# The recurrent loop of a layer: the LSTM moved to another phase of the step, with its high products ahead of the outer products, its gates ahead of tanh, its h ahead of the mask, and a copy by ScalarE

## The chip, the cores and the metric

The kernel runs on 1 core of one Trainium2 chip. The metric is the time of the device, in microseconds: the median of the kernel before is 2966.37 us over 3 runs (2957.95 to 2966.97).

The engines of the core are named as in the profile: PE (TensorE, matmuls), PEld (its weight loads), DVE (VectorE), ACT (ScalarE), POOL (GpSimd) and SP (SyncE, which here only issues DMAs). Each takes its instructions in the order in which they are written, and waits on semaphores.

## The reference

The kernel computes four layers on x of 8 sequences, 256 steps and 128 features. The change touches one stage of the third layer, which holds three recurrences over the 256 steps, each fed by the one before it:

```python
# L2_cond: LSTM, z = x Wx + b + h Wh, for each of 256 steps
i, f, o = sigmoid(ai), sigmoid(af), sigmoid(ao);  g = tanh(ag)
c = f * c + i * g
h = o * tanh(c)

# L2_attn: delta rule with 8 heads of 32, on xp = silu(h W_in^T)
kn        = k / (norm(k) + 1e-6)
delta     = v - S kn
S         = tanh(beta * S + outer(delta, kn))
Sq        = S q;   out = Sq * silu(Sq)        # y = out W_out^T, x = x + y

# L2_cond2: plain recurrence on the new x
h2 = tanh(h2 Wh2 + x Wx2 + b2)
```

## The kernel before

The stage is `recurrent_stages`. The 256 steps are cut into 16 waves of 16 steps (TC). The program runs in bodies of 16 steps: in body k the LSTM works on wave k, the projections (keys, values, beta, queries) on wave k-1, the delta rule on wave k-2, its output on wave k-3 and the plain recurrence (rnn) on wave k-4. So bodies 0 and 1 have the LSTM alone, bodies 2 to 15 have LSTM and delta rule, bodies 4 to 15 have everything, bodies 16 and 17 have the delta rule without the LSTM, and bodies 18 and 19 the rnn. The order on each engine is that of the program text: a loop over body and step on each engine, and inside it the calls of this step. What follows names lines of before.

- PE, a step of a full body: `retrieve` (L429, S times kn and q into `d_ps`), `rnn_product` (L406), `unread(o_ps)` (L448, a product that nobody reads), `spread_delta` (L441, the outer products into `o_ps`), `lstm_products` (L390, 24 bf16 products: h is split in three bf16 parts, the weights too), every eighth step a bias and the inputs of the rnn (L360, L400), `lstm_pieces` (L365, the inputs of the LSTM), `project` (L455 to L480), `output` (L490), `unread(d_ps)` (L448), `values` (L415, the v of the next step into `d_ps`).
- DVE: `masked` (L800, reads `d_ps`, writes `rows`; below a step is counted from the start of this instruction, called M), `lstm_h` (L772) and `split_h` (L785 to L794: h once more into PSUM, the rest, the middle part, the low part) for the LSTM step before, `summed` (L808, two halves), `project` and `output` (pieces of these stages), `lstm_cell` (L762, L765) for this LSTM step.
- ACT: `project` and `output`, `rnn_tanh` (L563), `new_state` (L556, two halves of S), `lstm_gates` (L546, L547), `lstm_tanh` (L551).
- POOL: `kept` (L649, beta times S, two halves), then pieces of `project` (norms, `kn_tok` L702, the spreading of kn and q L670).
- SP: for each body the stores of beta, kn and v to memory and their loads in another layout. `values` of a body's first step waits for `v_loaded`, the last part of this chain.

Of the kernel before, what the change touches and what calls it, by code (L numbers as in the profile page):

```python
# [9 lines left out]
BF16 = mybir.dt.bfloat16  # L10
ALU = mybir.AluOpType
# [7 lines left out]
P = 128  # L19
# [241 lines left out]
def recurrent_stages(nc, tag, x, y, wx, wh, bias, w_in, w_tok, w_q, beta_bias, w_out, sel_v, mask_r, mask_k, mask_q, mask_l, gate_sel,  # L261
# [8 lines left out]
    with ExitStack() as stack:  # L270
# [3 lines left out]
        h_rest, h_mid, h_low = mem.sb("h_rest", [P, WIDE]), mem.sb("h_mid", [P, WIDE], BF16), mem.sb("h_low", [P, WIDE], BF16)  # L274
# [34 lines left out]
                 "cell_ready", "tanh_ready", "h_ready", "rest_ready", "h_psum", "rest_psum", "mid_h_ready", "low_ready", "xin_psum", "xp_sig_ready", "xp_ready",  # L309
# [20 lines left out]
        def rnn_at(n, count=1):  # L330
            half, slot = (1, n % TC - 1) if 1 <= n % TC <= TCH else (0, (n - TCH - 1) % TC)
            at = (4 * TCH + slot) * B
            return lstm_ps[half][:, at:at + count * B]
# [18 lines left out]
        with nc.Block() as block:  # L352

            @block.tensor
            def _(pe):
# [14 lines left out]
                def lstm_pieces(w, step, rnn):  # L370
# [9 lines left out]
                def lstm_products(n):  # L380
                    alone = n <= IN_BANK
                    if not alone:
                        pe.wait_ge(s["low_ready"], n + 1)
                    h_parts = high(h_ring[:, (n - 1) % SLOTS, :]), high(h_rest[:, :]) if alone else h_mid[:, :], h_low[:, :]
                    for m in range(3):
                        if alone:
                            pe.wait_ge(s[("h_ready", "rest_ready", "low_ready")[m]], n + 1)
                        for g in range(4):
                            for k in range(3 - m):
                                last = nc.tensor.matmul(lstm_at(n, g, g + WIDE // B), w_part[k][:, g * P:(g + 1) * P],  # L390
                                                        h_parts[m], start=False, stop=(m == 2), skip_group_check=True)
                    last.then_inc(s["gates_psum"], 1)

                def rnn_inputs(w, lo, hi):
                    if lo == 0:
                        pe.wait_ge(s["x_added"], w + 1)
                        pe.wait_ge(s["r_ready"], w * TC + 1)
                    if lo == 1:
# [2827 lines left out]
```

## Time and profile before

| | |
|---|---|
| median of 3 runs | 2966.37 us |
| profiled execution | 2981.45 us, of which the span is 2979.7 us |
| mean granted TensorE clock | 0.821 |
| busy | PE 83%, PEld 59%, DVE 58%, ACT 37%, POOL 25% of the span |
| the stage of the change | about 1255 to 2180 us of the span |

The span runs from the first to the last instruction. The slices of the page show PE busy at 8 or 9 tenths through this stage, with the granted clock at 9 (full) up to about 2085 us and at 5 to 6 after it. PE's busy time counts pipelined matmuls from start to modelled end, so it isn't PE at its peak. The chain that the page follows back from the end lies in the last layer and says nothing on this stage.

### The profile page before, as it was taken

What the parts mean: (1) busy time and instruction counts of PE and PEld (TensorE: products, weight loads), DVE (VectorE), ACT (ScalarE), POOL (GpSimd) and SP (SyncE); (2) the same over time, 40 slices, a digit from 0 to 9 for tenths busy, and PEclk for the clock granted to TensorE, in tenths of its full rate; (3) what the DMA queues carried; (4) which work ended last, traced back from release to release, by engine and by line L of the source; (5) the groups of instructions that cost most, each with busy time, mean ns of one, the idle gap of its engine ahead of it and who ended that gap; (6) DMA issues with size and microseconds to landing.
All of it is one profiled execution on the core that took longest, in us unless ns stands there. A gap on an engine that the chain in (4) does not pass through costs nothing. (4 is left out here: it accounts for less than half of the span.)

```text
span 2979.7 us, 92693 instructions
## 1 busy us (share of the span) xinstructions
PE 2485.5 (83%) x37349; PEld 1762.4 (59%) x37354; DVE 1725.2 (58%) x7330; ACT 1105.3 (37%) x3986; POOL 750.8 (25%) x1227
## 2 busy tenths in 40 slices
PE   5998888882799889778888888889956878999998
PEld 3556666662455566555666666665534556777774
DVE  3553555556354544347777877776343865566675
ACT  1332333333133223224555555555244433333332
POOL 2210000000221000126666666767333310000000
PEclk9996555555699779889999999999556975898999
DMA  2000000001000000123534343435010000000000
GB/s 89 2 3 2 2 2 2 2 2 39 1 2 2 1 0 0 67 48 92 111 95 108 97 106 98 107 96 115 30 43 1 2 1 2 2 3 2 2 3 15
DMA packets 110106, 103.98 MB, mean 35 GB/s; under 512 B 90496, under 2 KB 90496, under 8 KB 108800
## 3 DMA queue, kind: packets, MB, share of 16 engines
q1 hardware_dynamic: 109696, 98.24, 13.1%
q8 instruction: 291, 4.77, 0.7%
q14 instruction: 119, 0.97, 0.1%
HBM read 89.81 MB, written 8.39 MB: 33 GB/s over the span
## 5 line engine op out<-in xcount | busy, mean ns | idle before, releaser
L649 POOL TENSOR_TENSOR l2r_beta_s<-l2r_state,l2r_beta_f 128x256 f32<-128x256 f32 x512 | 366.1, 736 | 274.8 <-ACT l2r_state L556 265.4
L556 ACT ACTIVATE l2r_state<-l2r_pre 128x256 f32<-128x256 f32 x512 | 191.6, 417 | 220.3 <-DVE l2r_pre L808 218.6
L808 DVE TENSOR_TENSOR l2r_pre<-l2r_o_ps,l2r_beta_s 128x256 f32<-128x256 f32 x512 | 193.1, 418 | 35.2 <-PE l2r_o_ps L441 33.1
L140 PE MATMUL l0r_bank<-main_x,l0r_wx_half 128*128 128x32 f32 (+2 forms) x480 | 150.0, 413 | 60.5 <-ACT l0r_out_gate L196 59.9
L140 PEld LDWEIGHTS l0r_bank<-main_x,l0r_wx_half 128*128 128x128 f32 x480 | 118.7, 311 | 81.7 <-ACT l0r_out_gate L196 79.5
L1801 PEld LDWEIGHTS l3r_bank<-main_x,l3r_wx_half 128*128 128x128 f32 x480 | 98.1, 231 | 93.2 <-issue 49.4
L441 PE MATMUL l2r_o_ps<-l2r_rows,l2r_outer 32*128 32x128 f32 x2048 | 134.1, 333 | 4.6 <-DVE l2r_rows L800 4.1
L194 ACT ACTIVATE l0r_gates<-l0r_bank 128x24 f32<-128x24 f32 x256 | 48.9, 191 | 237.0 <-PE l0r_bank L152 237.0
L1940 ACT ACTIVATE l3r_gates<-l3r_bank 128x24 f32<-128x24 f32 x256 | 48.9, 191 | 232.2 <-PE l3r_bank L1813 232.1
L228 DVE SCALAR_TENSOR_TENSOR l0r_both<-l0r_gates 128x16 f32<-128x16 f32 x256 | 44.8, 175 | 152.4 <-ACT l0r_gates L194 152.4
L152 PE MATMUL l0r_bank<-l0r_h_ring,l0r_w_part 128*128 128x8 bf16 x2304 | 102.6, 170 | 35.7 <-DVE l0r_h_ring L238 28.0
L1784 POOL TENSOR_SCALAR main_y<-l3r_h_ring 128x128 f32<-128x128 f32 x16 | 8.5, 530 | 481.9 <-DVE l3r_h_ring L2094 481.9
L152 PEld LDWEIGHTS l0r_bank<-l0r_h_ring,l0r_w_part 128*128 128x128 bf16 x2304 | 81.5, 105 | 68.4 <-DVE l0r_h_ring L238 65.0
L124 POOL TENSOR_SCALAR main_y<-l0r_h_ring 128x128 f32<-128x128 f32 x16 | 10.3, 645 | 441.8 <-DVE l0r_h_ring L238 441.8
L800 DVE TENSOR_TENSOR l2r_rows<-l2r_d_ps,main_even_layers 128x128 f32<-128x128 f32 x257 | 74.8, 291 | 80.5 <-PE l2r_d_ps L429 75.4
L448 PE MATMUL l2r_d_ps<-l2r_w_part 128*128 128x384 bf16 x384 | 120.8, 359 | 0.0
L441 PEld LDWEIGHTS l2r_o_ps<-l2r_rows,l2r_outer 32*128 32x128 f32 x2048 | 83.5, 191 | 55.5 <-DVE l2r_rows L800 48.0
L429 PE MATMUL l2r_d_ps<-l2r_state,l2r_kq 128*32 128x128 f32 x2056 | 114.2, 284 | 1.6 <-ACT l2r_state L556 1.4
L2084 DVE SCALAR_TENSOR_TENSOR l3r_both<-l3r_gates 128x16 f32<-128x16 f32 x256 | 44.4, 173 | 114.1 <-ACT l3r_gates L1940 113.3
L1314 DVE TENSOR_REDUCE l1a_block_top<-l1a_s_ps 128x6 f32<-128x768 f32 x64 | 61.3, 958 | 83.1 <-PE l1a_s_ps L1167 83.1
L1801 PE MATMUL l3r_bank<-main_x,l3r_wx_half 128*128 128x32 f32 (+2 forms) x480 | 95.9, 295 | 15.4 <-ACT l3r_out_gate L1942 14.8
L1314 DVE TENSOR_REDUCE l0a_block_top<-l0a_s_ps 128x6 f32<-128x768 f32 x64 | 61.3, 958 | 79.6 <-PE l0a_s_ps L1167 79.6
(590 smaller groups left out, 7305.4 us busy)
## 6 DMA issues: line engine op xcount, KB each, us to landing
l2r_beta_f<-l2r_beta_store SPq DMA_DIRECT2D x256, 256.0 KB, 3.3
main_odd_layers<-in_l SPq DMA_DIRECT2D x1, 4826.5 KB, 14.1
main_odd_layers<-in_l SPq DMA_DIRECT2D x1, 3672.0 KB, 16.3
l2r_v_store<-l2r_v_part SPq DMA_DIRECT2D x32, 96.0 KB, 3.5
l2r_v_rows<-l2r_v_store SPq DMA_DIRECT2D x16, 192.0 KB, 7.0
main_decay<-in_decay SPq DMA_DIRECT2D x1, 3072.0 KB, 10.2
main_even_layers<-in_l SPq DMA_DIRECT2D x1, 2762.5 KB, 9.7
l2r_beta_store<-l2r_beta_tok SPq DMA_DIRECT2D x128, 16.0 KB, 1.6
```

The source lines that it names most:

```text
L140: nc.tensor.matmul(into, wx_half[:, g * P:(g + 1) * P], x_b[:, :, w * LW + lo:w * LW + hi].rearrange("p b t -> p t b"), start=False, stop= ...
L152: last = nc.tensor.matmul(ifg(n, at, at + 1), w_part[part][:, g * P:(g + 1) * P], h_parts[k], start=False, stop=(k == 2), skip_group_check ...
L194: nc.scalar.activation(gates[:, 0:3 * B], ifg(n), ACT.Tanh).then_inc(s["gates_ready"], 1)
L429: last = nc.tensor.matmul(d_ps[chunk_rows(c), 0:P], kq[:, n % SLOTS, c, :, :, :].rearrange("p a b c -> p (a b c)"), state[:, c * P:(c + 1) ...
L441: last = nc.tensor.matmul(o_ps[:, c, 0:P], outer[chunk_rows(c), n // TC % 2, n % TC, :, :].rearrange("p a b -> p (a b)"), rows[chunk_rows( ...
L448: nc.tensor.matmul(into[:, P:CHUNK], w_part[0][:, 0:P], w_part[0][:, 0:3 * P], start=True, stop=True)
L556: nc.scalar.activation(state[:, h * 2 * P:(h + 1) * 2 * P], pre[:, h * 2 * P:(h + 1) * 2 * P], ACT.Tanh).then_inc(state_ready[h], 1)
L649: nc.gpsimd.tensor_tensor(beta_s[:, half].rearrange("p (g r) -> p g r", g=HG), state[:, half].rearrange("p (g r) -> p g r", g=HG), beta_f[ ...
L800: nc.vector.tensor_tensor(rows[:, n % SLOTS, :, :].rearrange("p a b -> p (a b)"), d_ps[:, 0:P], mask_r, ALU.mult).then_inc(s["row_ready"], 1)
L808: nc.vector.tensor_tensor(pre[:, half].rearrange("p (c n) -> p c n", c=2), o_ps[:, 2 * h:2 * h + 2, 0:P], beta_s[:, half].rearrange("p (c ...
L1314: nc.vector.tensor_reduce(block_top[:, :, 2 * p:2 * p + 2, r].rearrange("p n g -> p g n"), s_ps[:, :, 0:SPAN].rearrange("p g (n k) -> p g ...
L1801: nc.tensor.matmul(into, wx_half[:, g * P:(g + 1) * P], x_b[:, :, w * LW + lo:w * LW + hi].rearrange("p b t -> p t b"), start=False, stop= ...
```

## The change

Nothing is computed otherwise, but for the parts of h: the middle part is now the upper half of `h_rest` in SBUF and has no tile of its own. The calls of a step stand in another order on PE, DVE and ACT, and the copy of h into PSUM goes from DVE to ACT.

```diff
 # PE, a step
                         if delta is not None or final:
                             retrieve(n)
-                        if rnn is not None:
-                            if step == 0:
-                                rnn_inputs(rnn, 0, 1)
-                            rnn_product(rnn * TC + step)
+                        if lstm is not None:
+                            lstm_high(lstm * TC + step, None if rnn is None else rnn * TC + step)
                         if delta is not None:
-                            unread(o_ps[:, 0, :])
+                            if lstm is None:
+                                unread(o_ps[:, 0, :])
                             spread_delta(n)
                         if lstm is not None:
-                            if rnn is not None and step in (0, TCH):
-                                pe.wait_ge(s["r_ready"], rnn * TC + step + 2)
-                            lstm_products(lstm * TC + step)
+                            lstm_rest(lstm * TC + step)
...
                         if lstm is not None:
                             lstm_pieces(lstm, step, rnn)
+                        if rnn is not None:
+                            rnn_product(rnn * TC + step)
 # PE, the products in three parts
+                def lstm_high(n, rnn_steps):
+                    if rnn_steps is not None:
+                        pe.wait_ge(s["r_ready"], rnn_steps + 1)
+                    pe.wait_ge(s["h_ready"], n + 1)
+                    gate_products(n, 0)
+                def lstm_rest(n):
...
+                    pe.wait_ge(s["low_ready"], n + 1)
+                    if n > IN_BANK:
+                        gate_products(n, 1)
+                    gate_products(n, 2)
 # ACT, a step
+                def copy_h(n, rnn):
+                    act.wait_ge(s["h_ready"], n + 2)
+                    if rnn is None:
+                        act.wait_ge(s["d_psum"], n - IN_BANK + 1)
+                    nc.scalar.activation(parts_at(n, 0), h_ring[:, n % SLOTS, 0:B], ACT.Identity).then_inc(s["h_psum"], 1)
...
-                        if rnn is not None:
-                            rnn_tanh(rnn * TC + step)
+                        if lstm is not None:
+                            lstm_gates(lstm * TC + step)
                         if delta is not None:
                             new_state(delta * TC + step)
                         if lstm is not None:
-                            lstm_gates(lstm * TC + step)
                             lstm_tanh(lstm * TC + step)
+                        if rnn is not None:
+                            rnn_tanh(rnn * TC + step)
+                        if lstm is not None and IN_BANK <= lstm * TC + step < T - 1:
+                            copy_h(lstm * TC + step, rnn)
+                        later, at = divmod(k * TC + step + 1, TC)
+                        _, proj, _, out, _ = waves(later)
+                        # then project(proj, at) and output(out, at), which stood at the step's start
 # DVE, split_h
-                    nc.vector.tensor_tensor(lstm_at(n, 3, 4), lstm_at(n, 2, 3), tanh_c[:, :], ALU.mult)
-                    nc.vector.tensor_tensor(rest, lstm_at(n, 3, 4), high(h_ring[:, n % SLOTS, 0:B]), ALU.subtract)
-                    nc.vector.tensor_copy(h_mid[:, 0:B], high(rest))
-                    nc.vector.tensor_tensor(h_low[:, 0:B], rest, h_mid[:, 0:B], ALU.subtract)
+                    dve.wait_ge(s["h_psum"], n - IN_BANK + 1)
+                    nc.vector.tensor_tensor(parts_at(n, 1), parts_at(n, 0), high(h_ring[:, n % SLOTS, 0:B]), ALU.subtract)
+                    nc.vector.tensor_tensor(h_rest[:, 0:B], parts_at(n, 0), high(h_ring[:, n % SLOTS, 0:B]), ALU.subtract)
+                    nc.vector.tensor_tensor(h_low[:, 0:B], parts_at(n, 1), high(h_rest[:, 0:B]), ALU.subtract)
 # DVE, a step: masked, split_h, summed, lstm_cell, project, output (add_out at step 15), lstm_h
 # SP, a body
                     if proj is not None:
+                        store_kn(proj)
                         store_beta(proj)
-                        store_kn(proj)
+                        load_kn(proj)
                         store_v(proj)
-                        load_kn(proj)
```

The diff is cut: semaphore increments of `split_h` and the bank arithmetic of `rnn_at` and `parts_at` are left out. The addition of the output to x (`add_out`), which stood at the start of the next body's first step, stands in step 15 of its own body.

PE, step 4 of body 11, a full body. `l2r_d_ps` takes S kn and S q, `l2r_o_ps` the outer products, `l2r_lstm_psa` and `psb` the gates; `w_part` on `w_part` is the unread product. Before:

```order
L429 MATMUL l2r_d_ps<-l2r_state,l2r_kq 32x128 x4
L406 MATMUL l2r_lstm_psb<-l2r_r_ring,main_even_layers 128x8
L448 MATMUL l2r_o_ps<-l2r_w_part 128x384
L441 MATMUL l2r_o_ps<-l2r_rows,l2r_outer 128x128 x4
L390 MATMUL l2r_lstm_psa<-l2r_h_ring,l2r_w_part 128x56 x12
L390 MATMUL l2r_lstm_psa<-l2r_h_mid,l2r_w_part 128x56 x8
L390 MATMUL l2r_lstm_psa<-l2r_h_low,l2r_w_part 128x56 x4
```

and the same place in the changed kernel:

```order
L442 MATMUL l2r_d_ps<-l2r_state,l2r_kq 32x128 x4
L388 MATMUL l2r_lstm_psa<-l2r_h_ring,l2r_w_part 128x56 x12
L454 MATMUL l2r_o_ps<-l2r_rows,l2r_outer 128x128 x4
L388 MATMUL l2r_lstm_psa<-l2r_h_rest,l2r_w_part 128x56 x8
L388 MATMUL l2r_lstm_psa<-l2r_h_low,l2r_w_part 128x56 x4
L369 MATMUL l2r_lstm_psb<-main_x,main_even_layers 128x8x8
L419 MATMUL l2r_lstm_psb<-l2r_r_ring,main_even_layers 128x8
```

The twelve products with the high part of h (`h_ring`) moved ahead of the outer products, the product of the rnn (`r_ring`) behind the LSTM's, and the unread product into `o_ps` is gone.

ACT, step 5 of the same body. `state` is S, `cand_cell` the candidate and the cell, `r_ring` the state of the rnn. Before:

```order
L563 ACTIVATE l2r_r_ring<-l2r_lstm_psb,main_even_layers 128x8
L556 ACTIVATE l2r_state<-l2r_pre 128x256 x2
L546 ACTIVATE l2r_lstm_psa<-l2r_lstm_psa 128x24
L547 ACTIVATE l2r_cand_cell<-l2r_lstm_psa 128x8
L551 ACTIVATE l2r_tanh_c<-l2r_cand_cell 128x8
```

and in the changed kernel:

```order
L556 ACTIVATE l2r_lstm_psa<-l2r_lstm_psa 128x24
L557 ACTIVATE l2r_cand_cell<-l2r_lstm_psa 128x8
L572 ACTIVATE l2r_state<-l2r_pre 128x256 x2
L561 ACTIVATE l2r_tanh_c<-l2r_cand_cell 128x8
L579 ACTIVATE l2r_r_ring<-l2r_lstm_psb,main_even_layers 128x8
L567 ACTIVATE l2r_lstm_psb<-l2r_h_ring 128x8
L599 ACTIVATE l2r_v_tok<-l2r_m_ps 128x256
```

The two gate instructions stand ahead of the state, the tanh of the rnn and the copy of h behind it, and the projection's instruction last.

## Rows read from the trace of the kernel before

**Rows 1.** Window of body 17; PE, PEld, DVE, ACT, POOL busy, clock, DMA, GB/s

```profile
2084.00:2143.00 59.00, 59.00 (x432) 31.23 (x431) 22.16 (x58) 17.38 (x50) 22.20 (x32) 0.51 0.14 42
```

**Rows 2.** Line L800 (masked) in bodies 4 to 15: count, durations, first and last start

```profile
L800 DVE TENSOR_TENSOR l2r_rows<-l2r_d_ps,main_even_layers x192: 279/292/293, 1432.6 to 2035.4; 128x128 f32<-128x128 f32 x192
```

**Rows 3.** Timeline, steps 2 to 4 of body 11: start, length, engine, line

```profile
1793.47 0.29 DVE L800 TENSOR_TENSOR l2r_rows<-l2r_d_ps,main_even_layers 128x128 f32<-128x128 f32 x1 [0.29 <-PE l2r_d_ps L429]
...
1794.65 0.49 PE L390 MATMUL l2r_lstm_psa<-l2r_h_ring,l2r_w_part 128*128 128x56 bf16 x12 [0.33 <-DVE l2r_h_low L794]
...
1794.97 0.37 PE L390 MATMUL l2r_lstm_psa<-l2r_h_mid,l2r_w_part 128*128 128x56 bf16 x8
...
1795.18 0.26 PE L390 MATMUL l2r_lstm_psa<-l2r_h_low,l2r_w_part 128*128 128x56 bf16 x4
...
1796.60 0.29 DVE L800 TENSOR_TENSOR l2r_rows<-l2r_d_ps,main_even_layers 128x128 f32<-128x128 f32 x1 [0.29 <-PE l2r_d_ps L429]
...
1799.51 0.29 DVE L800 TENSOR_TENSOR l2r_rows<-l2r_d_ps,main_even_layers 128x128 f32<-128x128 f32 x1
```

**Rows 4.** Timeline, one step of body 16, without the LSTM

```profile
2049.62 0.29 DVE L800 TENSOR_TENSOR l2r_rows<-l2r_d_ps,main_even_layers 128x128 f32<-128x128 f32 x1 [0.45 <-PE l2r_d_ps L429]
...
2050.00 0.50 PE L441 MATMUL l2r_o_ps<-l2r_rows,l2r_outer 32*128 32x128 f32 x8
...
2050.43 0.49 PE L466 MATMUL l2r_m_ps<-main_even_layers,l2r_xp 128*128 128x128 f32 x2
...
2051.03 0.75 ACT L556 ACTIVATE l2r_state<-l2r_pre 128x256 f32<-128x256 f32 x2 [0.83 <-DVE l2r_pre L808]
...
2051.83 0.14 PEld L429 LDWEIGHTS l2r_d_ps<-l2r_state,l2r_kq 128*32 128x32 f32 x4 [0.19 <-ACT l2r_state L556]
...
2052.29 0.29 DVE L800 TENSOR_TENSOR l2r_rows<-l2r_d_ps,main_even_layers 128x128 f32<-128x128 f32 x1 [0.45 <-PE l2r_d_ps L429]
```

**Rows 5.** Timeline, one step of body 1, the LSTM alone

```profile
1302.79 0.27 PE L390 MATMUL l2r_lstm_psa<-l2r_h_low,l2r_w_part 128*128 128x56 bf16 x4
...
1303.10 0.17 ACT L546 ACTIVATE l2r_lstm_psa<-l2r_lstm_psa 128x24 f32<-128x24 f32 x1 [1.10 <-PE l2r_lstm_psa L390]
1303.18 0.17 ACT L547 ACTIVATE l2r_cand_cell<-l2r_lstm_psa 128x8 f32<-128x8 f32 x1
...
1303.39 0.18 DVE L762 TENSOR_TENSOR l2r_lstm_psa<-l2r_lstm_psa,l2r_cand_cell 128x16 f32<-128x16 f32 x1 [0.26 <-ACT l2r_cand_cell L547]
...
1303.81 0.21 ACT L551 ACTIVATE l2r_tanh_c<-l2r_cand_cell 128x8 f32<-128x8 f32 x1 [0.46 <-DVE l2r_cand_cell L765]
...
1304.05 0.17 DVE L772 TENSOR_TENSOR l2r_h_ring<-l2r_lstm_psa,l2r_tanh_c 128x8 f32<-128x8 f32 x1 [0.27 <-ACT l2r_tanh_c L551]
```

**Rows 6.** Timeline of DVE, step 5 of body 7: the projection's two instructions

```profile
1602.50 0.41 DVE L822 TENSOR_REDUCE l2r_ssq<-l2r_k_sq 128x8 f32<-128x256 f32 x1
1602.94 0.59 DVE L825 TENSOR_SCALAR l2r_guess<-l2r_ssq 128x8 int32<-128x8 int32 x1
```

**Rows 7.** Timeline of POOL, body 11, steps 8 and 9

```profile
1813.71 1.42 POOL L649 TENSOR_TENSOR l2r_beta_s<-l2r_state,l2r_beta_f 128x256 f32<-128x256 f32 x2
1815.08 0.62 POOL L702 TENSOR_TENSOR l2r_kn_tok<-l2r_k_tok,l2r_inv 128x256 f32<-128x256 f32 x1
```

**Rows 8.** Timeline of SP's queue, body 11, from step 9

```profile
1815.08 3.70 SPq L939 DMA_DIRECT2D l2r_beta_store<-l2r_beta_tok  x8
1818.88 1.26 SPq L948 DMA_DIRECT2D l2r_kn_store<-l2r_kn_tok  x2
...
1822.99 1.71 SPq L957 DMA_DIRECT2D l2r_kn_rows<-l2r_kn_store  x4
...
1826.69 0.37 SPq L976 DMA_DIRECT2D l2r_v_rows<-l2r_v_store  x1
```

**Rows 9.** DMA issues of body 11: KB each, median us to landing

```profile
l2r_v_rows<-l2r_v_store SPq DMA_DIRECT2D x1, 192.0 KB, 7.5
```

**Rows 10.** Timeline, edge of bodies 16 and 17: first values of body 17

```profile
2083.09 0.10 PEld L415 LDWEIGHTS l2r_d_ps<-l2r_v_rows,l2r_selv_bf 128*32 128x32 bf16 x4 [2.01 <-DMA l2r_v_rows<-l2r_v_store]
```

More of the change, by code:

```diff
@@ L273, in recurrent_stages @@
         h_ring = mem.sb("h_ring", [P, SLOTS, WIDE])
-        h_rest, h_mid, h_low = mem.sb("h_rest", [P, WIDE]), mem.sb("h_mid", [P, WIDE], BF16), mem.sb("h_low", [P, WIDE], BF16)
+        h_rest, h_low = mem.sb("h_rest", [P, WIDE]), mem.sb("h_low", [P, WIDE], BF16)
         w_part = [mem.sb(f"w_part{n}", [P, 4 * P], BF16) for n in range(3)]
@@ L330, in rnn_at, with parts_at @@
         def rnn_at(n, count=1):
-            half, slot = (1, n % TC - 1) if 1 <= n % TC <= TCH else (0, (n - TCH - 1) % TC)
-            at = (4 * TCH + slot) * B
-            return lstm_ps[half][:, at:at + count * B]
+            at = (4 * TCH + n % TCH) * B
+            return lstm_ps[1 - n % TC // TCH][:, at:at + count * B]
+        def parts_at(n, which):
+            at = (5 * TCH + which) * B
+            return lstm_ps[1 - (n + 1) % TC // TCH][:, at:at + B]
         def steps(wave, lo=0, hi=TC):
@@ L375, in lstm_pieces @@
                         if rnn is not None:
-                            pe.wait_ge(s["r_ready"], rnn * TC + step + 2)
+                            pe.wait_ge(s["r_ready"], rnn * TC + step + 1)
                         for g in gates:
                             lstm_inputs(w, half, g)
[L380 to L392, printed above, removed]
@@ L394, in rnn_inputs, with gate_products @@
-                def rnn_inputs(w, lo, hi):
+                def gate_products(n, m):
+                    h_part = (high(h_ring[:, (n - 1) % SLOTS, :]), high(h_rest[:, :]), h_low[:, :])[m]
+                    for g in range(4):
+                        for k in range(3 - m):
+                            last = nc.tensor.matmul(lstm_at(n, g, g + WIDE // B), w_part[k][:, g * P:(g + 1) * P], h_part,
+                                                    start=False, stop=(m == 2), skip_group_check=True)
+                    if m == 2:
+                        last.then_inc(s["gates_psum"], 1)
@@ L627, in _ @@
                     for step in range(TC):
-                        if proj is not None:
-                            project(proj, step)
-                        if out is not None:
-                            output(out, step)
-                        if rnn is not None:
-                            rnn_tanh(rnn * TC + step)
+                        if lstm is not None:
+                            lstm_gates(lstm * TC + step)
                         if delta is not None:
@@ L636, in _ @@
                         if lstm is not None:
-                            lstm_gates(lstm * TC + step)
                             lstm_tanh(lstm * TC + step)
+                        if rnn is not None:
[4 more added lines that the diff above has]
+                        _, proj, _, out, _ = waves(later)
+                        if proj is not None:
+                            project(proj, at)
+                        if out is not None:
+                            output(out, at)
             @block.gpsimd
@@ L907, in _ @@
                             output(out, step)
+                            if step == TC - 1:
+                                add_out(out)
                         if lstm is not None:
-                            lstm_cell(before + 1)
-                            if before + 1 < IN_BANK:
-                                lstm_h(before + 1)
-                                split_alone(before + 1)
+                            lstm_h(here)
+                            if here < IN_BANK:
+                                split_alone(here)
             @block.sync
```

53 lines of the change are left out of this document (23 added, 30 removed).

## The prediction

> **What bounds the kernel now.** I read the granted clock and the busy times by body first, then the starts of one instruction that comes once a step, then the timeline of single steps, last the DMA queue. The page's chain from the end lies in the last layer, so the stage has to be read from its own waits. A step is counted from masked to masked (M). Over the 192 steps of bodies 4 to 15 it lasts (2035.4 - 1432.6) / 191 = 3.156 us [rows 2], so a full body 50.5 us. Two steps in a row last 3.13 and 2.91 us [rows 3]. They differ by one fp32 product on PE, so such a product costs 0.22 us and PE's queue is in the loop: M, then DVE does h, its PSUM copy, rest, middle and low part, and PE's 24 LSTM products start 1.18 us after M because they wait for the low part; 0.53 us later the last four start, and 1.42 us after that comes the next M, with the pieces, the unread product, the values and the retrieval in between [rows 3]. So the step is 1.18 + 0.53 + 1.42 = 3.13 us, serial from end to end: the LSTM's splitting on DVE is ahead of its products, and all else of PE is behind them.
>
> What the step would be without the LSTM is to be seen in body 16 [rows 4]: M, outer products at +0.38, the next group on PE at +0.81, ACT's state at +1.41, the second half of the retrieval at +0.80 after the state's start, M again 0.46 later. That is 1.41 + 0.80 + 0.46 = 2.67 us, the loop of the delta rule alone, and no step can be faster after the change. What the LSTM alone needs is in body 1 [rows 5]: last four products to sigmoid 0.31, candidate 0.08 later, cell 0.21, tanh 0.42, h 0.24.
>
> **PE and ACT, the new step.** The twelve high products go into the gap in which PE waits for the mask. In [rows 3] they take 0.32 us, and between the second half of the retrieval and the outer products lie 0.46 + 0.38 = 0.84 us [rows 4], so they fit if h is there in time. The unread product went with them. On DVE three instructions are left between mask and low part instead of five, since h is copied by ACT one step earlier. The low part then comes at about M + 0.7, before PE is through with the outer products, so the remaining twelve products start at M + 0.81 [rows 4] instead of after the low part. The last four start 0.21 later, M + 1.02 [rows 3], sigmoid at + 1.33, candidate at + 1.41 [rows 5]. The state stands behind them on ACT. ACT starts a ready instruction about 0.09 before the end of the one ahead (the candidate 0.08 after a sigmoid of 0.17, [rows 5]), so the state starts at M + 1.50 and not at 1.41. Then 0.80 + 0.46 as in body 16: the step is 2.76 us. Below, this is bounded by 2.67 (gates free). Above: the gates could come later than in body 1, since no row shows the remaining products directly behind outer products; 0.15 us more gives 2.91. I take 2.76, as every part has its row.
>
> Does the LSTM keep up? Cell at 1.41 + 0.21 = 1.62, ready for tanh at 2.04, but ACT works on the state until 1.50 + 0.75 = 2.25; tanh at 2.16, h at 2.40, PE can start the high products at about 2.65, when the retrieval is through, and h's copy on ACT ends about 2.85, when DVE comes to it at 2.76 + 0.2. So it keeps up with 0.1 to 0.2 us to spare. That margin is thin, and h now stands on DVE behind `project` and `output`, which were ahead of the cell before. An instruction of 0.6 us there is hidden (1.84 + 0.6 = 2.44), more is not. In step 5 the two instructions take 0.44 + 0.59 [rows 6], h comes 0.4 late and the outer products of the next step, behind the high ones on PE, 0.28 late. Step 8, with three short ones, I put at 0.16, step 1 at 0.08.
>
> **PE's own queue** is the second bound: rest at 0.81, last group 0.21 later, then of the 1.42 us to the next M those two products out and the rnn's product in: 0.81 + 0.21 + 0.98 + 0.22 = 2.22 us plus 0.22 for each fp32 product. Two products give 2.66 and are hidden, three (steps 12 and 13) give 2.88, + 0.12 each; step 0 with bias, rnn inputs and projection counts as 3.3, 2.95, + 0.19; step 8 + 0.05. POOL has 1.42 us for beta times S each step [rows 7] and the spreading behind it in steps 11 to 14, some 1.4 to 1.7 us, more than a step together; with the slack it has I put 0.2 us beyond the former. Sum of one body: 16 x 2.76 + 0.28 + 0.16 + 0.08 + 0.19 + 0.05 + 0.24 + 0.20 = 45.4 us.
>
> **The DMA chain** is what is late next. Before, SP starts the stores of step 9 at 1815.08, issues v's load at 1826.69, and it lands 7.5 us later, at 1834.2, 19.1 us from the start [rows 8, 9]. From step 9 to the next body's first M are seven steps, 22.1 us, so it is in time. In the shorter body, with seven steps of 2.76, or 19.3 us, it isn't. M of step 9 comes at 9 x 2.76 + 0.76 = 25.6 us. The chain starts now with kn, which POOL makes behind its pair of 1.42 us [rows 7]; with the pair starting at about M - 0.5 the kn is stored from M + 1.5 on. v's store now stands behind the load of kn too, 1.71 + 0.15 us further back [rows 8], but v's load waited before for its place behind four loads of beta and not for this store, so I add no more than 1.8 and as little as -0.8 (the beta loads go out earlier) and take 19.0 us. v lands at 25.6 + 1.5 + 19.0 = 46.1, and M is 0.5 after it: 46.6 us for a body, 1.2 of it waiting at its edge. In return the load of kn is early, and ACT's outer instructions don't wait.
>
> **The sum.** Bodies 4 to 15: 12 x (50.5 - 46.6) = 47 us less. Bodies 2 and 3, which have no rnn (the copy of h waits there for the retrieval, ending about M, in time for DVE) and a start of the delta rule that the change doesn't touch: 2.5 us each, 5 us. Bodies 0 and 1: the LSTM alone, the same operations, 0. Body 16: its chain is 1 us longer, + 1. Body 17 is bound by PE at half clock and the sum of PE's work stays, 0. Together -51 us against the profiled execution's own 2981.45, of which 1.75 lie outside the span: 2930. The profiled execution is 0.5% above the median of 2966.37; the loss is in the loop and not in what differs between runs, so I take the same 51 off: 2915. Nearly all small terms that I left out (a semaphore more, DVE coming late to the mask) lengthen the step, and 224 steps make 0.02 us into 4.5; I name 2918 us.
>
> **The clock.** In body 17 PE is busy for all of 59.00 us, with a granted clock of 0.51 [rows 1]: the lower level, 1.2 GHz, though it never rests. It fell as PE had waited 2.01 us for v [rows 10]. The Trainium skill ("TensorE: Matmul & The Clock Gate", section "What's actually happening") says that the low level is the default and that activity releases it. By that rule body 17 should be back at 2.4 GHz at once, and 16 steps of 2.67 would take 43 us; the trace disagrees, busy alone doesn't bring it back. The sum doesn't use this rule.
>
> **The rivals.**
> 1. The step goes to about 2.91 instead of 2.76, by late gates or by an h that is late behind DVE's extras. For it: the margins of 0.1 to 0.2 us and DVE's fuller queue. Against it: each offset has its row. A body is then 16 x 2.91 + 0.8 + wait, about 48.3, and 12 x 2.2 + 4 = 30 us less: 2936. Chance 0.24.
> 2. The edges cost no wait (v lands at the low bound, 18.2) and the clock holds over body 17: body 45.5 and 16 x 2.67 = 43 against 59 us. 2918 - 13 - 16 = 2889. For it: the fall needs a wait at one edge only; against: body 16's own chain is longer. Chance 0.10.
> 3. Slower: the clock falls at the edge of every body. Before, only body 16 was short enough to wait, 2.01 us, and it fell there; now all 14 bodies wait, and the unread product that filled PE in every step is gone. Price: a step of body 17 takes 59 / 16 = 3.7 us at the low level, and with 24 LSTM products (0.53 + 0.08 at the high one, twice that) about 4.5, so 1.7 more than 2.76. Two such steps a body take back 3.4 of 3.9 us; it decides from the third on. With four, 6.8 us a body: 14 x (6.8 - 3.8) = + 42, 3008. Against it: the wait expected is 1.2 us, and the full step has more on PE than body 17's. Chance 0.12.
> 4. The step is shorter but something that isn't in the order (the load of v at its upper bound of 20.8, a wait of ACT in the projection) holds a body near 50 us: 2960 to 2972, no gain. Chance 0.07.
>
> **How the numbers follow.** Forecast 0.47, at 2918. Its own range is 2900 to 2934 (step 2.70 to 2.83, chain 18.2 to 20.8). The range of 8 in 10 takes in rivals 1 and most of 2: 2890 to 2960. A change of 0.3%, 9 us, is what the measurement can tell. Faster: 0.47 + 0.24 + 0.10 = 0.81; same: 0.07; slower: 0.12.
>
> **What would show it.** In the profile after, the mask's line starts every 2.7 to 2.85 us in full bodies; the high products start right behind the retrieval and end before the outer products; ACT's gates start at M + 1.33 and the state 0.17 later; PE has a wait for v's load of about 1 us at each edge; kn's load is no longer waited for; the clock stays at 1.00 to body 16 and is 0.5 in body 17. I am wrong if the high products wait for h regularly, if the state starts later than M + 1.6, if steps 5 and 8 aren't the long ones, or if the clock has rows of 0.5 in bodies 3 to 15.

## The result and the profile after

The changed kernel takes 3025.33 us, the median of 4 runs (2979.51 to 3037.26), against 2966.67 of before in the same comparison: a ratio of 1.0143 with a 95% interval of 1.0081 to 1.0205. The interval lies above 1, so the change makes the kernel slower, by 0.8 to 2%, where 2918 with a range to 2960 was forecast. The time of this kernel goes with its granted clock (2979.51 us at 0.802, 3022.14 at 0.778, 3037.26 at 0.776); the profiled execution is the longest, so its low stretches stand here at the upper end of what the runs show, and what is compared below is its bodies with each other.

First the same line as in [rows 2], masked, now L817, bodies 4 to 15.

```profile
L817 DVE TENSOR_TENSOR l2r_rows<-l2r_d_ps,main_even_layers x192: 278/292/293, 1433.3 to 2077.6; 128x128 f32<-128x128 f32 x192
```

(2077.6 - 1433.3) / 191 = 3.373 us a step instead of 3.156. The mean hides two kinds of steps; the windows by body show them. These are bodies 4 to 10, then 15, 16 and 17 (the columns are those of [rows 1]; the last three are clock, DMA share and GB/s).

```profile
1433.00:1481.00 48.00, 44.25 (x818) 32.36 (x810) 35.56 (x162) 27.93 (x128) 33.66 (x61) 1.00 0.49 113
1481.00:1543.00 62.00, 61.83 (x826) 44.95 (x819) 35.89 (x162) 27.51 (x127) 33.50 (x63) 0.61 0.34 83
1543.00:1590.00 47.00, 44.21 (x816) 32.37 (x813) 35.37 (x163) 27.62 (x127) 34.63 (x63) 1.00 0.44 103
1590.00:1649.00 59.00, 56.64 (x817) 41.30 (x813) 35.70 (x162) 27.87 (x127) 34.02 (x62) 0.71 0.39 89
1649.00:1706.00 57.00, 54.60 (x822) 39.77 (x817) 36.12 (x165) 27.92 (x127) 34.00 (x62) 0.76 0.39 90
1706.00:1759.00 53.00, 49.85 (x797) 36.46 (x798) 35.32 (x160) 27.93 (x127) 34.00 (x62) 0.84 0.42 94
1759.00:1814.00 55.00, 52.37 (x827) 37.96 (x819) 35.87 (x163) 27.90 (x127) 34.00 (x62) 0.81 0.41 96
...
2032.00:2082.00 50.00, 46.45 (x801) 33.44 (x798) 35.45 (x162) 27.44 (x126) 34.02 (x62) 0.93 0.45 103
2082.00:2146.00 64.00, 63.87 (x456) 35.04 (x455) 24.12 (x66) 20.75 (x63) 33.82 (x62) 0.51 0.33 81
2146.00:2205.00 59.00, 59.00 (x441) 30.05 (x433) 22.45 (x59) 15.56 (x50) 22.21 (x32) 0.50 0.14 42
```

Where the clock is 1.00 a body takes 47 or 48 us, against 50.2 to 50.9 before. Elsewhere it takes up to 62. The work of PE is the same (about 820 products); what changes is the clock column. The next view is the timeline of the last step of body 8, at the edge to body 9, the counterpart of [rows 3, 4, 10].

```profile
1701.23 0.39 PEld L388 LDWEIGHTS l2r_lstm_psb<-l2r_h_ring,l2r_w_part 128*128 128x128 bf16 x12 [0.22 <-ACT l2r_r_ring L579]
...
1701.33 0.29 DVE L817 TENSOR_TENSOR l2r_rows<-l2r_d_ps,main_even_layers 128x128 f32<-128x128 f32 x1 [0.21 <-PE l2r_d_ps L442]
...
1701.67 0.50 PE L454 MATMUL l2r_o_ps<-l2r_rows,l2r_outer 32*128 32x128 f32 x8
...
1702.11 0.38 PE L388 MATMUL l2r_lstm_psb<-l2r_h_rest,l2r_w_part 128*128 128x56 bf16 x8
...
1702.63 0.17 ACT L556 ACTIVATE l2r_lstm_psb<-l2r_lstm_psb 128x24 f32<-128x24 f32 x1 [0.66 <-PE l2r_lstm_psb L388]
...
1702.78 0.81 ACT L572 ACTIVATE l2r_state<-l2r_pre 128x256 f32<-128x256 f32 x2
...
1703.68 1.41 POOL L670 TENSOR_TENSOR l2r_beta_s<-l2r_state,l2r_beta_f 128x256 f32<-128x256 f32 x2 [1.00 <-DMA l2r_beta_f<-l2r_beta_store]
...
1705.11 0.10 PEld L428 LDWEIGHTS l2r_d_ps<-l2r_v_rows,l2r_selv_bf 128*32 128x32 bf16 x4 [1.93 <-DMA l2r_v_rows<-l2r_v_store]
```

In this last step the new order is as it was meant: high products right behind the retrieval, outer products 0.34 after M, the other twelve LSTM products at M + 0.78, the sigmoid at M + 1.30, the state at M + 1.45. (In most other steps it is not quite so; see the part on why the prediction was wrong.) Then PE waits 1.93 us for v. And this is the clock around that edge:

```profile
1690.00:1702.00 12.00, 11.83 (x228) 9.17 (x227) 8.32 (x41) 8.64 (x35) 12.00 (x22) 1.00 0.63 126
1702.00:1705.00 3.00, 1.46 (x27) 1.07 (x19) 1.60 (x7) 1.39 (x7) 2.00 (x3) 1.00 1.06 191
1705.00:1708.00 3.00, 2.89 (x50) 2.31 (x51) 1.95 (x9) 0.99 (x6) 0.43 (x2) 0.91 0.93 198
1708.00:1711.00 3.00, 3.00 (x39) 1.77 (x39) 0.97 (x7) 0.60 (x3) 1.07 (x2) 0.50 0.32 98
1711.00:1726.00 15.00, 14.94 (x186) 11.02 (x183) 8.81 (x38) 6.03 (x30) 5.46 (x9) 0.55 0.18 55
1726.00:1729.00 3.00, 2.73 (x54) 1.91 (x54) 2.55 (x13) 1.34 (x8) 1.64 (x3) 1.00 0.33 90
```

PE is half idle in the second row, busy again in the third, and in the fourth the clock is down from 2.4 to 1.2 GHz. In the 18 us from there on PE is busy nearly all the time, mostly at the low level, with steps of 4.1 to 4.5 us instead of 2.8. Such waits for v stand at 14 of the 15 edges between bodies 1 and 16 (1.48 to 4.31 us). The clock was low already when the first began; of the other 13, 12 are followed by a fall. The edge without a wait is that into body 6: body 5 was at the low level for 48 us, so slow that v was there in time, and body 6 is the fast one, 47.1 us.

By bodies, the profiled executions differ as follows: bodies 2 and 3 -2.6 us, bodies 4 to 15 +42.9 (648.7 against 605.8), body 16 +19.2 (64.4 against 45.2), body 17 -0.9, together 58.6. A body of this kernel at full clock with nothing to wait for takes 45.8 us (e6 below). With that, the +42.9 of bodies 4 to 15 are 12 x (45.8 - 50.5) = -56 for the shorter step, +22 for the waits (last steps of more than 2.78 us), and the rest, +77, for steps at the low clock.

Why v is late: SP's queue in body 10, from step 9, whose M is 1792.34 (against [rows 8, 9]).

```profile
1793.65 1.71 SPq L964 DMA_DIRECT2D l2r_kn_store<-l2r_kn_tok  x2
1795.53 3.81 SPq L955 DMA_DIRECT2D l2r_beta_store<-l2r_beta_tok  x8
1799.45 1.77 SPq L973 DMA_DIRECT2D l2r_kn_rows<-l2r_kn_store  x4
1801.38 1.93 SPq L984 DMA_DIRECT2D l2r_v_store<-l2r_v_part  x2
1803.47 2.13 SPq L943 DMA_DIRECT2D l2r_beta_f<-l2r_beta_store  x4
1806.21 0.31 SPq L992 DMA_DIRECT2D l2r_v_rows<-l2r_v_store  x1
```

kn's store starts 1.31 after M, v's load goes out 12.56 later, and PE takes up v at 1813.10, 6.9 after that. The load goes out when v's store has landed, 12.54 after the start of kn's store; the last of the four loads of beta ahead of it was issued by 11.95. From M of step 9 to the next body's M are 21.56 us; over bodies 4 and 6 to 14 it is 21.0 to 23.1.

### The profile page after: what moved, and what is told of

Its sections match the earlier page's. It is cut to its first block and busy times, and to the rows that moved or that the text cites. A ratio compares the mean times of both kernels' runs of the same rounds, so it can differ in the third digit from the quotient of the medians.

```text
span 3035.5 us, 92386 instructions
## 1 busy us (share of the span) xinstructions
PE 2583.5 (85%) x37098; PEld 1844.3 (61%) x37098; DVE 1680.1 (55%) x7106; ACT 1105.4 (36%) x4210; POOL 754.2 (25%) x1226
## 5 line engine op out<-in xcount | busy, mean ns | idle before, releaser
L817 DVE TENSOR_TENSOR l2r_rows<-l2r_d_ps,main_even_layers 128x128 f32<-128x128 f32 x257 | 74.9, 292 | 152.7 <-PE l2r_d_ps L442 147.3
L454 PE MATMUL l2r_o_ps<-l2r_rows,l2r_outer 32*128 32x128 f32 x2048 | 157.1, 384 | 0.2
L442 PE MATMUL l2r_d_ps<-l2r_state,l2r_kq 128*32 128x128 f32 x2056 | 154.5, 329 | 1.5 <-ACT l2r_state L572 1.1
L461 PE MATMUL l2r_d_ps<-l2r_w_part 128*128 128x384 bf16 x384 | 137.6, 407 | 0.0
L454 PEld LDWEIGHTS l2r_o_ps<-l2r_rows,l2r_outer 32*128 32x128 f32 x2048 | 98.7, 227 | 26.7 <-DVE l2r_rows L817 12.6
L556 ACT ACTIVATE l2r_lstm_psa<-l2r_lstm_psa 128x24 f32<-128x24 f32 x128 | 22.4, 175 | 239.7 <-PE l2r_lstm_psa L388 239.7
L1829 PE MATMUL l3r_bank<-l3r_h_ring,l3r_w_part 128*128 128x8 bf16 x2304 | 99.1, 168 | 7.7 <-DVE l3r_h_ring L2110 5.1
```

The costliest lines, as they stand in the source:

```text
L442: last = nc.tensor.matmul(d_ps[chunk_rows(c), 0:P], kq[:, n % SLOTS, c, :, :, :].rearrange("p a b c -> p (a b c)"), state[:, c * P:(c + 1) ...
L454: last = nc.tensor.matmul(o_ps[:, c, 0:P], outer[chunk_rows(c), n // TC % 2, n % TC, :, :].rearrange("p a b -> p (a b)"), rows[chunk_rows( ...
L461: nc.tensor.matmul(into[:, P:CHUNK], w_part[0][:, 0:P], w_part[0][:, 0:3 * P], start=True, stop=True)
L817: nc.vector.tensor_tensor(rows[:, n % SLOTS, :, :].rearrange("p a b -> p (a b)"), d_ps[:, 0:P], mask_r, ALU.mult).then_inc(s["row_ready"], 1)
L1829: last = nc.tensor.matmul(ifg(n, at, at + 1), w_part[part][:, g * P:(g + 1) * P], h_parts[k], start=False, stop=(k == 2), skip_group_check ...
```

## The experiments

**e1: v's store ahead.** SP's queue: kn store, v store, kn load, beta stores, v load, first beta load.

```
-                        store_beta(proj)
-                        load_kn(proj)
                         store_v(proj)
-                        load_beta(proj, 0, range(4), delta, 10)
+                        load_kn(proj)
+                        store_beta(proj)
                         load_v(proj)
+                        load_beta(proj, 0, range(4), delta, 10)
```

> The changed kernel with SP's order in a body made kn store, v store, kn load, beta stores, v load, beta loads; nothing else. Theory (the wait at the body's edge lets the clock fall, the low clock costs the time): v's load is issued some 9 us after the kn is ready instead of 13, no wait for it at the edges, granted clock 1.00 through bodies 3 to 15, bodies of about 45.7 us (the warm steps of the changed kernel added up) against 54, so 2966 - 57 - 5 = about 2900 us, 2885 if body 17 stays at the high clock too. Rival (the unread product that was taken out is what held the clock, waits or not): the clock still falls in most bodies, time above 2960 us.

Measured: 2950.26 us, ratio 0.996 (0.9917 to 1.0002). Waits for a DMA in bodies 4 to 17 (us in total, times, longest), one line in all:

```profile
POOL l2r_beta_s L670 <- DMA l2r_beta_f<-l2r_beta_store: 35.0, 14, 3.7
```

The wait for v is gone, and beta, whose stores and loads now come last, is waited for instead; the first step of a body lasts 3.4 to 5.1 us. The clock fell at 4 edges of bodies 3 to 16 (into 3, 8, 12 and 16), and for 3 us at a fifth, instead of 12. (The two traces are not alike: this one is the shortest of ten executions, that of the changed kernel the longest of four. Over all of them the mean granted clock is 0.792 to 0.819 against 0.776 to 0.802.) The falls into bodies 8 and 12 came at waits of PE of only 0.97 and 0.91 us, for a state that is held up by the late beta; a wait of 0.96 us in body 7 left the clock alone. A body with the clock held takes 46.0 to 47.6 us. The loss of the change is gone with the wait for v; the theory holds for the cause and not for the 2900.

**e2: the unread product kept.** In the changed kernel, also in steps with the LSTM.

```
-                            if lstm is None:
-                                unread(o_ps[:, 0, :])
+                            unread(o_ps[:, 0, :])
```

> The changed kernel with the unread product into o_ps left in every step, between the high products and the outer products; the edge waits stay. Theory of the edge wait: the clock still falls at edges where PE waits about 2 us for v, time 2980 to 3030 us, though a full step with more on PE may bring it back a step or two sooner. Rival (the missing unread product): the clock holds but for single windows, time below 2940 us. The product itself costs at most 0.16 us a step on PE where PE is the bound.

Measured: 3005.26, ratio 1.0186 (1.014 to 1.0232). Around its edge to body 12, where PE waits 1.88 us for v:

```profile
1833.00:1836.00 3.00, 3.00 (x48) 2.39 (x41) 2.25 (x10) 1.23 (x6) 0.66 (x1) 0.83 0.69 152
1836.00:1848.00 12.00, 12.00 (x136) 7.96 (x139) 5.40 (x25) 3.15 (x17) 3.59 (x6) 0.50 0.18 56
1848.00:1887.00 39.00, 36.69 (x656) 25.81 (x654) 27.56 (x127) 23.34 (x105) 29.73 (x56) 0.99 0.45 102
```

The clock still falls, so the missing product isn't the trigger. But it comes back sooner: in bodies 3 to 15 it is low for 95 us in all, against 244 in the changed kernel, and over all runs the mean granted clock is 0.798 to 0.813 against 0.776 to 0.802. The product costs 0.15 us in every step (2.95 instead of 2.80), so that nothing is won.

**e3: PE kept busy over the edge.** Ten unread products at the end of each body, ahead of the wait for v.

```
+                            if step == TC - 1:
+                                for _ in range(10):
+                                    unread(d_ps)
                             values(n + 1)
```

> The changed kernel with ten unread products more on PE at the end of a body, ahead of the wait for v's load (1.6 us of PE work at the high clock, in a wait of 1.5 to 3.3 us); the wait and all else stay. Theory of the edge wait: the clock holds in most bodies, which become 45.7 + 2 = 47.7 us, so about 2935 us (2920 to 2960). Rival (the missing product within the steps): no change from the changed kernel, about 3025 us.

Measured: 2948.29, ratio 0.9946 (0.9903 to 0.999). Bodies 5, 12 and 17:

```profile
1475.00:1522.00 47.00, 45.46 (x820) 33.12 (x820) 35.33 (x161) 27.71 (x127) 34.01 (x62) 1.00 0.42 102
1813.00:1883.00 70.00, 70.00 (x826) 50.70 (x826) 35.96 (x162) 27.39 (x127) 34.08 (x62) 0.54 0.29 72
2077.00:2119.00 42.00, 39.96 (x436) 21.32 (x432) 22.40 (x59) 15.27 (x49) 21.84 (x32) 1.00 0.24 67
```

v is still waited for, 0.92 to 1.76 us at seven edges into full bodies, but PE's own idle time there is 0.4 us shorter than the wait, and the last step is filled. In bodies 4 to 15 the clock is low in body 12 (behind a pause of 1.41 us at its start, which the profile gives to "issue": it shows nothing that PE waits for) and for 3 us in body 7, and the ratio goes from 1.0143 to 0.9946. Nothing inside a step was touched, so it is the idle time at the edge that makes the clock fall, and not the order inside the step. Body 17, 59 us in [rows 1], takes 42.

**e4: SP's queue as it was,** with the new order of work on PE, ACT and DVE.

```
-                        store_kn(proj)
                         store_beta(proj)
-                        load_kn(proj)
+                        store_kn(proj)
                         store_v(proj)
+                        load_kn(proj)
```

> The changed kernel with SP's order of before (beta stores, kn store, v store, kn load). Theory: v's store is 1.7 us earlier in the queue and the chain starts with beta, which is ready sooner than kn, so the wait for v is shorter by 0.5 to 1.5 us, 0.5 to 2 us instead of 1.5 to 3.3, and the clock falls at fewer edges: 2940 to 3000 us. But kn's load comes later and ACT waits for it in steps 12 and 13, about 1 us a body, which is a second idle place for PE; if that is what lets the clock fall, it is no better than 3000. Rival (the new order of SP has nothing to do with it): 3025 us.

Measured: 2936.83, ratio 0.9945 (0.9907 to 0.9982), a little below the range expected. PE waits for v at eight edges of bodies 4 to 15, 0.43 to 1.10 us. Five of these were followed by nothing. At the three where the clock fell, into bodies 9, 11 and 13 (0.45, 0.74 and 0.43 us), another pause of PE stands behind the wait. This is the one at 1667 (a weight load), and the clock around it:

```profile
1667.61 0.10 PEld L364 LDWEIGHTS l2r_lstm_psb<-l2r_gate_bf,l2r_bias_t 12*128 12x128 bf16 x1 [1.28 <-issue]
```

```profile
1665.00:1668.00 3.00, 1.83 (x41) 1.23 (x34) 2.24 (x10) 0.96 (x5) 1.59 (x4) 0.94 0.92 195
1668.00:1671.00 3.00, 3.00 (x31) 2.07 (x31) 0.34 (x3) 0.62 (x3) 0.53 (x1) 0.50 0.33 101
1671.00:1680.00 9.00, 9.00 (x108) 6.72 (x105) 4.88 (x23) 2.69 (x14) 2.83 (x4) 0.50 0.10 31
```

PE stands still for 1.28 us in the first step of the body, and nothing in the profile that it waits for ends it ("issue"). The others, at 1766.35 and 1865.00, are 1.27 and 1.13 us. The longest low stretch, 41 us from 1411.63, begins in step 13 of body 3, at a wait of PE of 1.30 us for the state, which ACT wrote late because it had waited 2.06 us for kn's load. Waits for kn are the remaining cost of this order: 14 times, 18.4 us, so the second idle place of the expectation is real and took the clock once.

e4 undoes one part of the change alone, the order of SP's queue, and the ratio goes from 1.0143 to 0.9945. In body 10 its chain starts 0.40 us after M of step 9, with beta, and not 1.31 after it, with kn. So what made the change slower is its new order of the queue, together with the shorter body.

**e5: v late in the kernel before.** The old order of work, with v's store behind the load of kn and the loads of beta.

```
                         store_kn(proj)
-                        store_v(proj)
                         load_kn(proj)
                         load_beta(proj, 0, range(4), delta, 10)
+                        store_v(proj)
                         load_v(proj)
```

> The kernel before with v's store moved behind kn's load and the four beta loads in SP's queue, so that v lands later (about 21 to 23 us after the chain's start instead of 19.1); the order on PE, ACT and DVE is that of before. Theory (an idle PE at the body's edge lets the clock fall, in whatever phase the LSTM stands): PE waits 0.5 to 2 us for v at the edges, and where the wait is over some 1.5 us the clock falls to 0.5 and the next steps take 4 to 4.6 us; time 2975 to 3020 us. Rival (only the new order of work makes the clock fall): the clock stays at 1.00 to body 15 and the time rises by the waits alone, 5 to 20 us, to 2960 to 2975.

Measured: 3047.60, ratio 1.0347 (1.0303 to 1.0391), above the range expected. Two edges, a wait of 1.59 us into body 8 and one of 2.31 into body 12, and the windows of these two bodies:

```profile
1646.87 0.10 PEld L415 LDWEIGHTS l2r_d_ps<-l2r_v_rows,l2r_selv_bf 128*32 128x32 bf16 x4 [1.59 <-DMA l2r_v_rows<-l2r_v_store]
...
1853.39 0.10 PEld L415 LDWEIGHTS l2r_d_ps<-l2r_v_rows,l2r_selv_bf 128*32 128x32 bf16 x4 [2.31 <-DMA l2r_v_rows<-l2r_v_store]
```

```profile
1647.00:1698.00 51.00, 44.93 (x828) 31.36 (x824) 39.11 (x178) 27.62 (x111) 33.37 (x62) 1.00 0.41 96
1853.00:1911.00 58.00, 50.55 (x832) 35.36 (x832) 39.40 (x178) 28.02 (x111) 33.76 (x62) 0.88 0.41 90
```

The old order loses its clock in the same way. From body 3 on, the seven waits of 0.49 to 1.59 us left it alone, and the eight of 1.66 to 3.96 us, which end with the wait into body 17, were all followed by a fall, in bodies 3 to 16 for 10 to 21 us. So nothing in the new order is needed for the fall.

**e6: an order of the queue that has all three in time.** The eight beta stores are split: two, kn store, v store, two, kn load, four, v load, then the loads of beta.

```
-                def store_beta(w):
+                def store_beta(w, lo, hi):
...
+                        store_beta(proj, 0, 2)
                         store_kn(proj)
-                        store_beta(proj)
-                        load_kn(proj)
                         store_v(proj)
-                        load_beta(proj, 0, range(4), delta, 10)
+                        store_beta(proj, 2, 4)
+                        load_kn(proj)
+                        store_beta(proj, 4, B)
                         load_v(proj)
+                        load_beta(proj, 0, range(4), delta, 10)
```

> The changed kernel with SP's order made 2 beta stores, kn store, v store, 2 beta stores, kn load, 4 beta stores, v load, beta loads, so that kn, v and beta are all due before they are wanted. Theory: no wait for v or kn, at most 1 us for beta at the edges, clock at 1.00 through bodies 3 to 15, bodies of 45.5 to 46.5 us, 2890 to 2915 us. Rival (the clock falls at random in this order of work): single stretches of low clock remain and the time is near that of the version with v first, 2930 to 2950 us.

Measured: 2904.45 us (2891.86 to 2937.94), ratio 0.9826 (0.9772 to 0.9879). This beats both kernels. Body 5, then 15 to 17:

```profile
1461.00:1506.00 45.00, 43.49 (x795) 31.79 (x795) 34.74 (x158) 27.74 (x127) 32.77 (x61) 1.00 0.44 109
...
1924.00:1984.00 60.00, 59.40 (x802) 43.30 (x801) 35.64 (x162) 27.22 (x128) 34.07 (x62) 0.63 0.37 91
1984.00:2028.00 44.00, 41.78 (x471) 24.41 (x469) 25.40 (x69) 21.68 (x67) 33.54 (x62) 1.00 0.45 111
2028.00:2070.00 42.00, 39.74 (x428) 21.23 (x424) 22.36 (x59) 15.22 (x49) 23.22 (x33) 1.00 0.23 69
```

Bodies 2 to 14 take 45.7 to 47.2 us (masked to masked), with no wait for v or kn; what is left is beta, 1.0 to 3.0 us of POOL's time, most of it in POOL's slack. Body 15 lost its clock for 44 us, which was not expected, after a pause of 0.55 us ("issue") in its first step.

**e7: the same queue in the kernel before,** to see what the queue is worth without the new order of work.

> The kernel before with the same order of SP (2 beta stores, kn store, v store, 2 beta stores, kn load, 4 beta stores, v load, beta loads) and nothing else. Theory (in bodies of 50.5 us the chain isn't in the way): the same time as before within 0.3% in bodies 2 to 15; body 16, which did wait 2 us, may lose its wait and body 17 keep the clock, so between 2940 and 2967 us. Rival (SP's order is what gains): 40 us or more less.

Measured: 2946.02, ratio 0.9985 (0.9958 to 1.0013). Bodies 11 and 17:

```profile
1774.00:1824.00 50.00, 44.61 (x826) 31.23 (x819) 38.78 (x176) 27.55 (x111) 33.41 (x62) 1.00 0.41 102
2068.00:2111.00 43.00, 40.68 (x442) 22.17 (x436) 22.42 (x60) 17.36 (x51) 23.61 (x34) 1.00 0.24 70
```

Bodies 3 to 14 stay at 50.2 to 50.8 us. Body 17 keeps its clock and takes 43 instead of 59, but over the runs that isn't told from no change. So of the 1.7% of e6 nearly all comes from the new order, once its data are in time.

**e8: e4 with six unread products at each edge.**

> The changed kernel with SP's order of before and six unread products (1 us of PE work) at each body's end ahead of the wait for v. Theory: the waits for v of 0.4 to 1.1 us are filled, the edges with a low clock (5 of 14 in the version without the fill) go down to one or none, and the wait for kn in step 12 of up to 1.4 us stays; 2905 to 2930 us. Rival (the edges aren't where the clock falls): same as without the fill, 2937 us.

Measured: 2921.77, ratio 0.9896 (0.9864 to 0.9929). Two low stretches are left in bodies 3 to 16 (1565 to 1620 and 1914 to 1927), behind pauses of 1.04 and 1.31 us in the first step, both "issue".

**e9: e6 with six unread products at each edge.**

> The changed kernel with SP's order of e6 (two beta stores, kn store, v store, two beta stores, kn load, four beta stores, v load) and six more unread products on PE at the end of each delta body, ahead of the wait for v, as in e8. My theory: TensorE's clock falls only where its queue stands still at an edge. e6 still lost 44 us of low clock from 1927 after a small wait for beta; PE's six products cover such a wait, so at most one low stretch is left over bodies 3 to 16, bodies stay at 45.7 to 47.5 us (the six products of 0.16 us add up to 1 us a body, 14 us in all, where nothing was waited for) and the time is 2890 to 2915, at or a little below e6's 2904. Rival: the clock also falls for reasons that have nothing to do with the edges (by chance, or by the load). Then low stretches of 10 to 60 us stay, their number as in e6, the six products only cost their 14 us, and the time is 2915 to 2935.

Measured: 2912.30 (2896.86 to 2945.24), ratio 0.9851 (0.9813 to 0.9888), not told from e6. Body 5 of the profiled execution, which is the one of 2945.24 us:

```profile
1463.00:1534.00 71.00, 70.72 (x822) 51.12 (x818) 35.98 (x161) 27.38 (x127) 34.34 (x63) 0.53 0.30 76
```

Three low stretches stayed (68, 20 and 24 us), where at most one was expected; this execution is the longest of the six, and the others, with mean clocks of 0.820 to 0.831 against 0.813, had less of it. In each the first step had a pause, of 0.47 us ("issue") in body 5, 0.92 (the state, held up by a late beta) in body 12 and 1.09 ("issue") in body 14; the products at the edge can't cover a pause that comes later. The time is in my theory's range, but the trace sides with the rival: part of the falls has nothing to do with the wait for v.

## Why the prediction was wrong

**Right: the length of the step.** Forecast 2.76 us; at full clock a body without waits takes 45.8 us (e6, body 5) against 45.4 forecast, and an ordinary step 2.78 to 2.80. In steps 13 to 15 and 0 of a body the offsets were the forecast ones: outer products at M + 0.34 (0.38), rest at + 0.78 (0.81), sigmoid at + 1.30 (1.33), state at + 1.45 (1.50).

**Not quite right: how it comes about.** In most other steps h doesn't keep up by the 0.1 to 0.2 us of the forecast. This is step 5 of body 6, at full clock:

```profile
1557.09 0.17 DVE L792 TENSOR_TENSOR l2r_h_ring<-l2r_lstm_psa,l2r_tanh_c 128x8 f32<-128x8 f32 x1
...
1557.35 0.29 DVE L817 TENSOR_TENSOR l2r_rows<-l2r_d_ps,main_even_layers 128x128 f32<-128x128 f32 x1
1557.37 0.39 PEld L388 LDWEIGHTS l2r_lstm_psa<-l2r_h_ring,l2r_w_part 128*128 128x128 bf16 x12 [0.34 <-ACT l2r_r_ring L579]
...
1557.80 0.31 PEld L454 LDWEIGHTS l2r_o_ps<-l2r_rows,l2r_outer 32*128 32x128 f32 x8
```

The retrieval is through, and the high products start 0.11 us after the end of h, behind M (the view names `r_ring`, which was ready at 1557.09, before h at 1557.26). So the outer products come at M + 0.45 and not at + 0.34, and in step 2 at + 0.63. In the two bodies of the changed kernel at full clock, 4 and 6, the outer products come later than M + 0.4 in 20 of 32 steps and the state later than M + 1.6 in 10; in e6, bodies 4 to 14, the state does so in 58 of 176. Two of the signs of being wrong, high products that regularly wait for h and a state behind M + 1.6, thus came true, though they cost only some hundredths of a us in an ordinary step and about 0.2 in steps 2 and 6. ACT also still waited for kn's load, 5 times, 2.4 us in bodies 4 to 15, where no wait was forecast.

Within the body the corrections were placed wrongly: step 5 takes 2.80 and not 3.04, step 0 takes 3.21 and not 2.95, steps 2 and 6 take 2.97; the sum is nearly the same.

**Mis-sized: the edge.** "46.6 us for a body, 1.2 of it waiting at its edge." The waits were 1.48 to 4.31 us. Seven steps after M of step 9 took 21.0 to 23.1 us, 21.9 in the mean, where 1.5 + 19.0 + 0.5 = 21.0 was forecast, which turned out to be the lower end. The term that was too small is the chain, from its first store to the landing of v: 19.0 us. It was taken from body 11 alone [rows 8, 9], where it is 19.1. Over bodies 4 to 15 of the kernel before it takes 18.9 to 20.8 us, 19.8 in the mean, and in the changed kernel, bodies 4 and 6 to 15, 19.1 to 20.9, again 19.8. So v's store behind kn's load added nothing to the whole chain; it stood in it before, between kn's store and kn's load:

```profile
1820.30 1.82 SPq L968 DMA_DIRECT2D l2r_v_store<-l2r_v_part  x2
```

What its new place did is that v's load now waits until this store has landed, in all eleven of these bodies, 0.1 to 1.0 us behind the last load of beta ahead of it. In the kernel before the store had landed before the last of those loads was issued, in all twelve bodies. M to kn's store was 1.31 against 1.5 in body 10, and from the landing of v to M it was 0.64 to 0.87 against 0.5. For time alone this was worth 22 - 14 = 8 us over bodies 4 to 15.

**Failed: the clock.** "The clock stays at 1.00 to body 16 and is 0.5 in body 17." That is the step that failed. The mechanism was written down as rival 3, priced at 3008 us (the measured ratio gives 2966.67 x 1.0143 = 3009; the median of the four runs is 3025.33), and given 0.12. Two reasons stood against it. "The wait expected is 1.2 us": e4 and e5 bear this out as far as it goes (waits for v up to 1.1 us into the full bodies of e4 and up to 1.59 in e5 left the clock alone; the waits of 0.91 and 0.97 us in e1 did not), so the mistake in the chain decided over the clock too. "The full step has more on PE than body 17's": this didn't protect it. The trace of the kernel before had the wait of 2.01 us into body 17 and a fall [rows 1, 10]. It had a second one that the prediction doesn't name: 1.97 us for v into body 2, after which the clock was 0.50 from 1331 to 1341. Two cases out of two should have carried more weight than 0.12, the more so as the wait's own upper bound (20.8 for the chain) was 3.0 us. The profile before gave everything to see this: a margin of 1.2 us on an estimated chain of 19, and behind it a price of 1.7 us for every step at the low level.

Two prices of the rivals don't follow from their own terms. A low step of rival 3 is 3.7 + 2 x 0.61 = 4.9 us by its sum and not 4.5; 4.1 to 4.5 was measured, so the 4.5 came out well by luck. And rival 4 with the chain at 20.8 has bodies of 46.6 + 1.8 = 48.4 us and not near 50, so about 2940 us and not 2960.

Rival 3 had four low steps a body as its case and "from the third on" as its condition: three or more came in 10 of the 14 bodies 2 to 15, eleven in body 5.

**Right side of the balance, wrong place.** Body 16 was put at + 1 and body 17 at 0. Body 17 stayed at the low level, as forecast (-0.9), and body 16 fell with it, + 19.2.

**Open.** What the pauses of 0.5 to 1.4 us in the first step of a body are, which the profile gives to "issue". In the changed kernel none over 0.62 us is seen. In e3, e4, e6, e8 and e9 there are eight of 1.04 us and more, and all but one (1.28 us, at 1739.89 in e6) were followed by a fall. Of the shorter ones, those of 0.47 (e9), 0.55 (e6) and 0.82 us (e1) were, and those of 0.65 (e1, e2) were not. Open is also why one low stretch ends after 15 us and another lasts a body; e2 shows only that more work on PE in each step makes them shorter.

## What to carry to other kernels

A shorter loop moves every fixed chain beside it closer to the end. Before a step is shortened, work out when each transfer of the next stage is issued and lands, and count every entry that the queue holds in front of it; here 1 to 2 us of lateness turned -56 us into +43. On TensorE the price of a short idle time isn't its length: a wait of some 1.5 us or more was followed, nearly each time (12 of 13 waits of 1.48 to 3.33 us in the changed kernel), by 7 to 48 us at half clock, and from body 16 on by far more, so look at the clock column beside every wait of PE, and either bring the data in time (e6, -1.7%) or keep PE busy over the wait (e3, e8).

## What the hardware showed that was not expected

- Half clock outlasts its cause by far. After 1.93 us of waiting PE was at 0.50 to 0.55 for 18 us while it was busy for all but 0.06 us of it, and in e3 it was busy for all of the 70 us of a body at 0.54. The Trainium skill ("TensorE: Matmul & The Clock Gate", section "What's actually happening") has activity release the low level; the traces show that being busy at that level may not do so for a whole body and more: in bodies 16 and 17 of the changed kernel PE was busy for 122.87 of 123 us, at 0.50 to 0.51.
- The limit between waits that matter and those that don't isn't sharp: 1.52 us left the clock alone in the changed kernel, and 1.48 us at another edge of it did not. Over all runs it lies wider apart: 0.91 us was followed by a fall (e1, body 12), and 1.73 us was not (e4, into body 17).
- Eight stores of 16 KB hold SP's queue for 3.8 us. In e6 they all still go ahead of v's load. What moved is v's store, far enough ahead that its landing isn't waited for, and the four loads of beta, which go behind v's load. So v's load goes out 9.6 us after the first store of the group in body 10 and 9.9 in body 11, instead of 12.6 in body 10 of the changed kernel.
